# A mixture-of-experts stage with 79 expert steps instead of 80, activations cut into 128 and 48 rows, and five down products instead of six

## What is computed

```python
def step(y, ew):
    wg, wu, wd, c = ew
    h = jax.nn.silu(xf @ wg.T) * (xf @ wu.T)      # 176 columns for each expert
    return (y + h @ wd.T * c[:, None], None)      # back to 256 columns
y, _ = lax.scan(step, y0, (Wg, Wu, Wd, coeff.T))
z = jax.nn.silu(xf @ Sg.T) * (xf @ Su.T) @ Sd.T   # shared expert, 352 columns
```

## Time and profile before

| | |
|---|---|
| median of 3 runs | 631.28 us (627.23 to 631.92) |
| span of the profiled execution | 630.8 us |
| PE busy | 520.9 us (83%) |
| PE weight loads busy | 490.1 us (78%) |
| DVE busy | 402.5 us (64%) |
| ACT busy | 279.1 us (44%) |
| POOL busy | 298.4 us (47%) |

### The profile page before, as it was taken

How to read it: one execution, slowest core, us unless ns; L and a number is a source line. 1 busy time by engine, 2 the same in 40 slices (tenths; PEclk the granted TensorE clock), 3 DMA queues, 4 the chain that set the end, 5 groups by cost and what they waited for, 6 DMA issues and landing times. The chain is left out here.

```text
span 630.8 us, 13294 instructions
## 1 busy us (share of the span) xinstructions
PE 520.9 (83%) x3587; PEld 490.1 (78%) x3588; DVE 402.5 (64%) x1154; ACT 279.1 (44%) x740; POOL 298.4 (47%) x337
## 2 busy tenths in 40 slices
PE   1597991899999999999853068799999999999897
PEld 0287891799998898898842057699998999998896
DVE  3697731323568768769777199677776777774543
ACT  1252542223644544635325274355554555553232
POOL 5644520200104446445566499634443444447893
PEclk9798996557999999999955559799999999999899
DMA  7135688427776458462275653244443444446931
GB/s 221 47 110 171 209 211 244 130 70 177 193 173 182 143 143 215 129 168 75 94 234 197 234 181 94 69 125 127 125 125 110 128 134 127 124 143 249 415 146 51
DMA packets 63668, 98.41 MB, mean 156 GB/s; under 512 B 10084, under 2 KB 48867, under 8 KB 62263
## 3 DMA queue, kind: packets, MB, share of 16 engines
q1 hardware_dynamic: 50504, 58.37, 34.3%
q0 software_dynamic: 9184, 32.66, 13.8%
q10 hardware_dynamic: 3918, 6.67, 3.3%
HBM read 60.84 MB, written 40.17 MB: 160 GB/s over the span
## 5 line engine op out<-in xcount | busy, mean ns | idle before, releaser
L1572 POOL DMA_INDIRECT ys_scr<-h,ids_st x60 | 61.6, 1027 | 73.5 <-DVE h L1626 71.2
L109 PE MATMUL GU<-gu_hi,xT 128*128 x320 | 86.9, 354 | 5.2 <-DVE lo L1655 3.1
L144 POOL DMA_INDIRECT xs_scr<-h,slot_u x64 | 62.4, 975 | 55.7 <-PE TB L1194 26.7
L109 PE MATMUL YP<-dn_hi,aT 88*128 x320 | 69.1, 308 | 4.9 <-DVE aT L1611 4.8
L1618 DVE TENSOR_TENSOR h_act<-GU,g_act 128x176 f32<-128x176 f32 (+1 forms) x96 | 35.5, 370 | 57.2 <-ACT g_act L1490 56.2
L1204 PE MATMUL O<-raw,prob 128*128 128x99 f32 x512 | 71.2, 289 | 0.0
L823 ACT ACTIVATE prob<-TB 128x512 f32<-128x512 f32 x64 | 38.2, 597 | 71.5 <-PE TB L1194 70.7
L1497 ACT ACTIVATE aT<-HT 88x256 fp32r<-88x256 f32 (+1 forms) x96 | 38.1, 398 | 69.5 <-PE HT L1728 69.4
L1204 PEld LDWEIGHTS O<-raw,prob 128*128 128x128 f32 x512 | 66.7, 205 | 0.0
L109 PEld LDWEIGHTS GU<-gu_hi,xT 128*128 128x128 f32 x320 | 54.3, 198 | 6.3 <-issue 6.3
L109 PEld LDWEIGHTS YP<-dn_hi,aT 88*128 88x128 f32 x320 | 49.1, 191 | 11.2 <-issue 7.2
(11 more groups left out here) (226 smaller groups left out, 1291.2 us busy)
## 6 DMA issues: line engine op xcount, KB each, us to landing
x_st<-xs_scr SPq DMA_DIRECT2D x80, 144.0 KB
dn_hi<-k_scr SPq DMA_DIRECT2D x48, 192.0 KB, 3.8
planes<-ys_scr POOLq DMA_DIRECT2D x8, 1024.0 KB, 17.4
k_scr<-k_ev SPq DMA_DIRECT2D x8, 768.0 KB, 4.8
dn_hi<-q_scr SPq DMA_DIRECT2D x24, 256.0 KB, 4.4
q_scr<-q_ev SPq DMA_DIRECT2D x8, 512.0 KB, 3.0
raw<-in_egu SPq DMA_DIRECT2D x8, 352.0 KB
raw<-in_x SPq DMA_DIRECT2D x36, 64.0 KB, 2.7
```

The lines of the kernel that those rows point to most:

```text
L109: mm = eng.matmul(out, a, b, start=(i + j == 0), stop=(i == len(pairs) - 1 and j == 2))
L144: eng.indirect_dma_start(T["xs_scr"], bass.IndirectOffsetOnAxis(ap=T["slot_u"][:, par, t % 2, k:k + 1], axis=0), T["h2"][:, row, :], None) ...
L1572: eng.indirect_dma_start(ys, bass.IndirectOffsetOnAxis(ap=ids_st[:, r:r + 1].bitcast(U32), axis=0), results(r % 8), None).then_inc(sent[q] ...
```

## The change

Five things change, all for the expert stage:

1. `UNROLL, HEAD, TAIL` become 24, 18, 13. The loop runs over two turns of 24, and 18 + 48 + 13 = 79 steps are run instead of 80. Since the number is odd now, the shared steps use the other buffer of each pair.
2. PE waits for single low halves (`s + 1` gate and up, `s - 1` down) up to step 15 and 17, all unrolled, and never for all 16 at once ahead of time. DVE makes the low halves of experts 5 to 15 in steps 0, 1, 3, 4, 5, 7, 8, 9, 11, 12, 13 (`LOW_STEPS`) instead of 0 to 10.
3. The 176 activations of a row are cut into 128 and 48 instead of 88 and 88. Both transposes now take 128 columns of `h_act`; columns 176 and up are zeros, written once by the memset (2x208 columns instead of 2x32).
4. The low part of the activations is made by two instructions (`a_lo_once`): 128 rows of block 0, and then 48 rows of block 1, which are written under the high ones, to rows 64 to 111 of the same block. The down weights of block 1 stand twice in memory, in rows 0 to 47 and again in rows 64 to 111.
5. `down` has five matmuls: three for block 0, one of 48 rows with the low weights, and one of 112 rows that does high by high and low by high of block 1 together. The tensors of the down weights have 128 rows instead of 88, so their loads, `split_hi` and `dn_low` cover 128 rows.

```diff
-UNROLL, HEAD, TAIL = 32, 12, 4
+UNROLL, HEAD, TAIL = 24, 18, 13
+LOW_STEPS = (0, 1, 3, 4, 5, 7, 8, 9, 11, 12, 13)
...
-    eng.dma_start(T["raw"][0:FH, at, W_GU:W_EXP], A["ed"][:, at].rearrange("p e k x -> p (e k x)")).then_inc(loaded, 16)
+    eng.dma_start(T["raw"][:, at, W_GU:W_EXP], A["ed"][:, at].rearrange("p e k x -> p (e k x)")).then_inc(loaded, 16)
...
             if runs(s, 1):
-                a_hi(s - 1, 1 - p2, FH, 2)
+                a_hi(s - 1, 1 - p2, P, 2)
...
+        def a_lo_once(w, p2):
+
+            eng.wait_ge(aT_hi, w + 1)
+            eng.tensor_tensor(aT[:, p2, 1, 0, :], HT[p2][:, 0:P], aT[:, p2, 0, 0, :].bitcast(F32), ALU.subtract)
+            eng.tensor_tensor(aT[TWICE:TWICE + FR, p2, 0, 1, :], HT[p2][0:FR, P:2 * P], aT[0:FR, p2, 0, 1, :].bitcast(F32),
+                              ALU.subtract).then_inc(aT_lo, 1)
...
-        eng.memset(h_act[:, :, SH_I:SH_K * P], 0.0).then_inc(h_zero, 1)
+        eng.memset(h_act[:, :, FI:SH_K * P], 0.0).then_inc(h_zero, 1)
...
             if runs(s, 1):
-                a_lo(s - 1, 1 - p2, FH, 2)
-            if isinstance(s, int) and LO_AHEAD + s < NE:
-                gu_low(LO_AHEAD + s)
+                a_lo_once(s - 1, 1 - p2)
+            if isinstance(s, int) and s in LOW_STEPS:
+                gu_low(LO_AHEAD + LOW_STEPS.index(s))
...
             eng.wait_ge(aT_lo, w + 1)
-            three(eng, YP[p2][:, 0:D],
-                  [(aT[0:FH, p2, 0, k, :], aT[0:FH, p2, 1, k, :], dn_of(dn_hi, e, k), dn_of(lo, e, k))
-                   for k in range(2)]).then_inc(y_mm, 1)
+            y, both = YP[p2][:, 0:D], TWICE + FR
+            eng.matmul(y, aT[:, p2, 0, 0, :], dn_of(dn_hi, e, 0), start=True, stop=False)
+            eng.matmul(y, aT[:, p2, 1, 0, :], dn_of(dn_hi, e, 0), start=False, stop=False)
+            eng.matmul(y, aT[:, p2, 0, 0, :], dn_of(lo, e, 0), start=False, stop=False)
+            eng.matmul(y, aT[0:FR, p2, 0, 1, :], dn_of(lo, e, 1, 2), start=False, stop=False)
+            eng.matmul(y, aT[0:both, p2, 0, 1, :], dn_of(dn_hi, e, 1, 1), start=False, stop=True).then_inc(y_mm, 1)
...
-            if isinstance(s, int) and s < HEAD:
-                eng.wait_ge(gu_lo, NE if s == HEAD - 1 else s + 1)
+            if isinstance(s, int) and s < NE:
+                eng.wait_ge(gu_lo, s + 1)
...
-            if isinstance(s, int) and 2 <= s < HEAD:
-                eng.wait_ge(dn_lo, NE if s == HEAD - 1 else s - 1)
+            if isinstance(s, int) and 2 <= s < NE + 2:
+                eng.wait_ge(dn_lo, s - 1)
             if runs(s, 2):
                 down(w - 2, p2, before)
             if runs(s, 1):
-                transpose_a(w - 1, 1 - p2, FH, 2)
+                transpose_a(w - 1, 1 - p2, P, 2)
...
-         "ed": np.ascontiguousarray(g["Wd"].reshape(NE, D, 2, FH).transpose(3, 0, 2, 1)),
+         "ed": down,
```

More of the change, by code:

```diff
@@ L20 @@
 NE, TOPK, FI = 16, 4, 176
-FH = FI // 2
+FR = FI - P
+TWICE = P // 2
 SH_I = 2 * FI
@@ L150, in split_hi @@
     eng.activation(T["gu_hi"][:, e, :], T["raw"][:, e, 0:W_GU], ACT.Copy).then_inc(T["w_hi2"], 1)
-    eng.activation(T["dn_hi"][0:FH, e, :], T["raw"][0:FH, e, W_GU:W_EXP], ACT.Copy).then_inc(T["w_hi2"], 1)
+    eng.activation(T["dn_hi"][:, e, :], T["raw"][:, e, W_GU:W_EXP], ACT.Copy).then_inc(T["w_hi2"], 1)
 def fill_up(nc, eng, A, T, low, high):
@@ L1407, in gu_of, with dn_of @@
         return tensor[:, bass.ds(e, 1), k * 2 * FI:(k + 1) * 2 * FI].rearrange("p o x -> p (o x)")
-    def dn_of(tensor, e, k):
+    def dn_of(tensor, e, k, rows=0):
         at = W_GU if tensor is lo else 0
-        return tensor[0:FH, bass.ds(e, 1), at + k * D:at + (k + 1) * D].rearrange("p o x -> p (o x)")
+        return tensor[0:(P, TWICE + FR, FR)[rows], bass.ds(e, 1), at + k * D:at + (k + 1) * D].rearrange("p o x -> p (o x)")
     def tile_of(scr, n):
@@ L1537, in _ @@
         for n in range(TILES):
-            gate(NS + n, n % 2, GU[0], SH_I)
+            p2 = (NS + n) % 2
+            gate(NS + n, p2, GU[0], SH_I)
             if n < TILES - 2:
-                x_hi(NS + n + 2, n % 2)
+                x_hi(NS + n + 2, p2)
             if n == 0:
-                a_hi(NS - 1, 1, FH, 2)
+                a_hi(NS - 1, 1 - p2, P, 2)
             else:
-                a_hi(NS + n - 1, 1 - n % 2, P, SH_K)
-        a_hi(NS + TILES - 1, 1, P, SH_K)
+                a_hi(NS + n - 1, 1 - p2, P, SH_K)
+        a_hi(NS + TILES - 1, (NS + TILES - 1) % 2, P, SH_K)
     @block.gpsimd
@@ L1581, in _ @@
         for p in range(2):
-            eng.wait_ge(sent[p], 32 + 16 * (NS // 2))
+            eng.wait_ge(sent[p], 32 + 16 * len([s for s in range(NS) if s // 2 % 2 == p]))
         for n, g in enumerate(LOADED):
@@ L1632, in keep_late @@
             eng.wait_ge(add_ld[n // 4], 16)
-            eng.tensor_tensor(to_add[:, n, :], YP[n % 2][:, 0:D], to_add[:, n, :], ALU.add).then_inc(z_late, 1)
+            eng.tensor_tensor(to_add[:, n, :], YP[(NS + n) % 2][:, 0:D], to_add[:, n, :], ALU.add).then_inc(z_late, 1)
         def add_late(n):
@@ L1638, in add_late @@
             eng.wait_ge(fold, 3 * (n - KEPT) + 3)
-            done = eng.tensor_tensor(to_add[:, n, :], YP[n % 2][:, 0:D], planes[:, n, 0, :], ALU.add)
+            done = eng.tensor_tensor(to_add[:, n, :], YP[(NS + n) % 2][:, 0:D], planes[:, n, 0, :], ALU.add)
             done.then_inc(final if n % 2 else z_late, 1)
@@ L1702, in _ @@
             if n == 0:
-                a_lo(NS - 1, 1, FH, 2)
+                a_lo_once(NS - 1, 1 - p2)
             else:
@@ L1708, in _ @@
         add_late(TILES - 2)
-        a_lo(NS + TILES - 1, 1, P, SH_K)
+        a_lo(NS + TILES - 1, p2, P, SH_K)
         add_late(TILES - 1)
@@ L1919, in host_layout @@
     g = {k.replace("L0_ffn_", "").replace("L0_attn_", "").replace("L0_", ""): np.asarray(v) for k, v in x.items()}
-    w = g["w_qkv"]
+    w, by_row = g["w_qkv"], g["Wd"].transpose(2, 0, 1)
+    down = np.zeros((P, NE, 2, D), np.float32)
+    down[:, :, 0], down[0:FR, :, 1], down[TWICE:TWICE + FR, :, 1] = by_row[0:P], by_row[P:], by_row[P:]
     a = {"x": g["x"][0], "c": np.ascontiguousarray(g["c"].reshape(KD, P).T),
```

21 lines of the change are left out of this document (11 added, 10 removed).

## The result

The changed kernel is slower. Its median is 649.58 us (645.66 to 654.62) against 631.35 us (627.23 to 631.92) for the kernel before; the ratio is 1.035 with a 95% interval of 1.030 to 1.040. The forecast was 632, with a range that ended at 638.

What follows compares the result with a forecast made beforehand. It took a chain over transposes, ACT, DVE and down product to bound the loop step, and DVE the first steps; +1.7 - 1.2 + 0.3 + 0.2 = +1.0 us on 630.8 gave 631.8, 632 as median, range 625.5 to 638.

Steps and rivals of the forecast that it cites:

- -0.12: Down product in the loop's chain: one matmul of 256 columns less saves 0.12 us a step.
- that line of the forecast: Steps after the first 17: 61 x 2.27 + 3.1 = 141.6 us against 139.88 before, +1.7.
- One rival: DVE's second instruction, moving partitions 0 to 47 to 64 to 111, is dearer; 0.1 us more gives 639 us; chance 0.11.
- The pair on DVE: Low part of activations: two DVE instructions without overlap take 0.60 us instead of 0.42, +0.18 in the chain.
- The chain rules the step: Loop step: transposes, ACT, DVE and down product fill its 2.21 us, with PE standing some 0.1 us for `a_lo`.
- The rival that PE was the bound after all: Loop steps gain the whole matmul: 2.09 us each, 11 us less, 621 us; chance 0.04.
- The first steps: Steps 0 to 17: 47.7 us against 48.93, -1.2, with DVE as the bound and pairs costing 0.28 a step.
- the entry into the loop: At step 18, counted within the first steps: 1.0 us, between 0 and 2.2.
- 8 steps at 3.19: First steps with a low half: DVE's 2.91 us plus 0.28 for the pair, 8 x 3.19 = 25.5 us.
- The wait of 3.13 us and the half clock behind it: First steps: PE's wait for the last low half and the slow clock after it go, together 6.9 us.
- The rival of a falling clock: First steps: PE's clock falls in 13 steps, +11 us, 643 us; chance 0.04.
- Small terms: Edits outside the steps: larger memset +0.3 us, larger down weight loads +0.2, the other buffer in shared steps 0.

Runs made afterwards that it cites:

- With 112 rows: Changed kernel with the fourth down product (high activations of block 1 by low weights) at 112 rows instead of 48; repeat run 629.02 us, ratio 0.995 to the kernel before.
- the one with 96 rows: Changed kernel with the fourth down product at 96 rows instead of 48; step 2.267 us, steps behind the first 17 141.91 us, median 653.72 us.
- the kernel with six products, high first: Kernel before with 79 steps, single waits, spread low halves, and the four down products with high activations first; 611.35 us, ratio 0.971.

## Why the prediction was wrong, point by point

**The step that failed** is the sentence "The rows of a matmul (48, 88, 112, 128) don't show as time", and the -0.12 that rested on it. The rows of before have matmuls of 88 and of 128 rows next to each other at no cost, and I carried that on to 48, for which there was no row, without a bound. One matmul less in the chain, the term at fault, was not -0.12 but -0.12 + 0.38 = +0.26. Over 61 steps the 0.38 are 23.2 us, and the rest came out at 164.11 where the forecast had 141.6: 22.5 more. With 112 rows it is 141.85. Everything else in that line of the forecast held: the step without the row change was 2.267 for a forecast 2.27. The rule on changing modes, quoted above, speaks directly against this edit, and I had not weighed it. I had leaned on the fact that a load's duration does not depend on its rows. That holds: 0.18 us for 48 rows, 0.19 for 128. The Trainium skill says the same in "TensorE: Matmul & The Clock Gate", section "LDWEIGHTS (loading the stationary operand)". But the cost is not in a duration, it is between two starts. One rival had the kernel slower by 1% or more, but by a dearer second DVE instruction, and that is not what came.

**The pair on DVE**: right, 0.59 for 0.60, and the partition of the write decides as said. The 48 rows save next to nothing there (0.28 us against 0.29), though two rows of the trace, which any line joins, could not have shown that. The Trainium skill's rule in "VectorE: DVE Perf Modes", section on the TRN2 errata, gives 0.258 us for 128 columns from PSUM, too low for the 0.29 measured. The step by it (2.22 us) is wrong, and the rows' 2.27 is right. The Trainium skill has another formula in the same section, for an fp32 `tensor_tensor`, (columns + 151) / 0.96 ns, which gives 0.291 us and agrees.

**The chain rules the step**: right. Cutting it with PE's work unchanged takes 0.27 us from a step (2.267 to 2.001). The rival that PE was the bound after all is dead for before: with the waits cut, six products take a step of 2.115, and the step was 2.21. My "some 0.1 us" of standing is 2.208 - 2.115 = 0.09.

**The first steps**: 46.42 us for a forecast 47.7, but by two errors that cancel in part, which is luck. The 48-row product cost some 1.6 to 2.5 here too: the two traces with 112 rows have 43.88 and 44.40 us, the one with 96 rows 44.83. So what I had worked out for these steps should be held against 44 to 45, and was 2.9 to 3.8 too much. 1.0 of it is the entry into the loop, which lies behind silu of step 17 and so falls into the rest. For what remains, the term at fault is 8 steps at 3.19, with the low half at 1.69 us: in those three traces no step from 4 to 16 took over 3.01 us from silu to silu. In the changed kernel the low half took:

```profile
380.16 0.89 DVE L1666 TENSOR_TENSOR lo<-raw,gu_hi 128x704 fp32r<-128x704 f32 x1
...
396.75 1.42 DVE L1666 TENSOR_TENSOR lo<-raw,gu_hi 128x704 fp32r<-128x704 f32 x1
...
402.43 0.91 DVE L1666 TENSOR_TENSOR lo<-raw,gu_hi 128x704 fp32r<-128x704 f32 x1
```

POOL's subtractions beside the second, and the last that POOL has:

```profile
396.14 1.28 POOL L1555 TENSOR_TENSOR lo<-raw,dn_hi 128x512 fp32r<-128x512 f32 x1
...
399.05 1.29 POOL L1555 TENSOR_TENSOR lo<-raw,dn_hi 128x512 fp32r<-128x512 f32 x1
```

The low half at 396.75 shares 0.67 us with POOL's (up to 397.42) and takes 0.51 longer than the one at 402.43, which shares none. The others of this trace fall in line: 1.10, 1.23 and 1.28 us long where 0.34, 0.47 and 0.52 are shared, each 0.76 us and the shared time. The 1.69 of before shared 0.93. So 1.69 was not the price of the instruction but of its overlap with POOL. In the second trace with 112 rows the six low halves up to 398 us share 0.34 to 0.74 and take 1.09 to 1.49. That they share less because the pair ahead makes them start later fits these rows, and it would give back most of the pair's +0.28; no run isolates it. I had this in the text only for steps 11 to 13, as up to -1.5.

**The wait of 3.13 us and the half clock behind it** went, as forecast: the granted clock is 0.98 over the first steps (1.00 from 373 us on), where it was 0.89, and 1.00 behind them. The rival of a falling clock did not come.

**Small terms**: the memset took 0.41 us, +0.30 on the earlier trace rows, as forecast.

```profile
361.48 0.41 DVE L1668 MEMSET h_act<- 128x416 f32 x1 [12.70 <-PEq L1876]
```

The other buffer in the shared steps cost nothing that shows: their 16 steps took 61.39 us for 61.02. Silu of step 0 came at 369.76 instead of 371.90; in the later runs, whose edits lie behind it, that point lay between 362.6 and 371.2 us, so I read nothing from it. The +0.2 for the larger loads can't be seen against that; no run isolates it.

**Balance**, from silu of step 0 to the end: 258.9 before, 249.5 with 79 steps, single waits and spread low halves, 256.2 and 256.6 with the new layout and pair but 112 rows, 281.0 with 48. So -9.4, +6.7, and +24.8. Of the -9.4, 1.5 is in the shared steps, and of the +6.7, 2.0; no term of the forecast explains these, and between the traces the 16 shared steps take 59.4 to 61.8 us. For this span the forecast had +0.5 (-1.2 and +1.7), to be held against -9.4 + 6.7 = -2.7; the +24.8 it did not have.

## What to carry to other kernels

Don't put a product of up to 64 rows between ones of 88 and more without a price for it: one of 48 or 64 rows cost 0.38 us more here, as much as three products of 256 columns, and one filled up to 96 or 112 rows (with zeros, or a term that does no harm) cost no more than its neighbours. When the trace of before lacks a size that the change brings in, bound its price explicitly; "no difference between 88 and 128" says nothing about 48. And where a chain over engines fills the step, split its wait before cutting instructions: one more semaphore took 16.8 us from silu of step 0 to the end (256.2 to 239.4). The medians, 629 and 605 us, differ by more; 8.6 us of that lie ahead of this point in the two traces, where the granted clock from 120 to 290 us was 0.91 and 0.97 and the kernels are the same. The product saved had been paid for by DVE's second instruction in the chain until then.

## What the runs showed that I had not expected

- A product of up to 64 rows between ones of 88 or more costs 0.19 us between starts on its way in and 0.19 on its way out, whether PE would have waited or not, and the profile counts it as busy. The sign of it is a fall in the busy share of weight loads (94% to 79%) at an unchanged share of PE.
- A subtraction of 704 columns on DVE takes 0.88 to 0.91 us with no subtraction on POOL beside it. Where POOL's (512 columns) had begun first, it is longer by the shared time, 1.69 with 0.93 shared. Where DVE's began first, it kept its 0.88, and POOL's took 1.58 instead of 1.29 (at 398.72 and 399.18 us in the kernel with six products, high first). POOL's indirect DMA in these steps is longer too; why stays open, since the second one here runs beside a low half as well:

```profile
397.58 1.45 POOL L1576 DMA_INDIRECT ys_scr<-h,ids_st  x1 [0.17 <-issue]
...
402.42 0.97 POOL L1576 DMA_INDIRECT ys_scr<-y_st,ids_st  x1 [0.94 <-DVE y_st L1637]
```

  The Trainium skill, in the section of "VectorE: DVE Perf Modes" on two Vector instructions named above, says that DVE's second read from SBUF goes through an interface shared with GpSimd. Both operands of the subtraction lie in SBUF, so that fits the traces; no run here was made to isolate it.
